# The destinations' rows of two message stages in a PSUM bank, and one bank for the transposes: a graph network kernel on one Trainium2 core

## The reference, cut to what matters

```python
# second layer (stage "msg1"): 16 features by 8 edge attributes
x_j = node_features[col]
m = jnp.einsum('ei,ej,ijh->eh', x_j, edge_attr_e3nn, W_msg_tp) * norm_msg_tp
m = jax.nn.silu(m)
m = m @ W_msg_lin * norm_lin
agg = jax.ops.segment_sum(m, row, num_segments=n_nodes)
...
# fourth layer (stage "msg3"): 16 attributes by 16 features
edge_mats = (edge_features @ kernel + bias).reshape(-1, d, d)
neighbors = node_features[pair_indices[:, 1]]
transformed = jnp.einsum('eij,ej->ei', edge_mats, neighbors)
aggregated = jax.ops.segment_sum(transformed, pair_indices[:, 0], num_segments=node_features.shape[0])
```

## Time and profile before

| | |
|---|---|
| median of three runs | 25,102.21 us (25,093.5 to 25,139.49) |
| the profiled execution's own time | 25,105.15 us |
| its span from first to last instruction | 25,103.4 us |
| granted TensorE clock over the span | 0.723 of 2.4 GHz |
| PE / PEld / DVE busy | 15,996.3 / 11,741.1 / 16,286.5 us |
| ACT / POOL busy | 3,853.7 / 18,136.2 us |
| stage msg1 | 9,523 to 12,890 us, 125 turns |
| stage msg3 | 20,834 to 24,655 us, 125 turns |

### The profile page before, as it was taken

The page is one execution under the profiler, slowest core; times in us unless marked ns, Lnnn a source line. Parts: engine busy times, 40 slices in busy tenths (PEclk is TensorE's granted clock), DMA queues, the critical chain, the costliest instruction groups (busy, mean ns, idle before and its releaser), DMA issues. The chain is left out here.

```text
span 25103.4 us, 351859 instructions
## 1 busy us (share of the span) xinstructions
PE 15996.3 (64%) x99053; PEld 11741.1 (47%) x99056; DVE 16286.5 (65%) x41450; ACT 3853.7 (15%) x8407; POOL 18136.2 (72%) x17443
## 2 busy tenths in 40 slices
PE   4211110266666647888853888888888838999993
PEld 3211110155555535666633454455545516777772
DVE  7679976177777726777761666666666645666664
ACT  0000000122222211111100111111111101222220
POOL 5777777677777737777753777777777767888884
PEclk7555555555555557888875889888888867888886
DMA  3211111011111101111120111111111120101012
GB/s 103 82 35 43 44 37 30 14 31 31 31 31 31 31 10 25 25 25 25 25 79 7 20 19 20 19 19 20 20 19 19 20 72 24 26 25 26 25 26 74
DMA packets 1007292, 810.94 MB, mean 32 GB/s; under 512 B 579829, under 2 KB 897503, under 8 KB 1003105
## 3 DMA queue, kind: packets, MB, share of 16 engines
q0 software_dynamic: 557728, 189.18, 6.0%
q1 hardware_dynamic: 348648, 290.30, 4.3%
q10 hardware_dynamic: 100800, 330.28, 3.4%
HBM read 414.80 MB, written 393.60 MB: 32 GB/s over the span
## 5 line engine op out<-in xcount | busy, mean ns | idle before, releaser
L1513 POOL DMA_INDIRECT msgs<-msg_msg,msg_pos x4875 | 5730.9, 1176 | 1550.8 <-issue 1485.0
L1748 POOL DMA_INDIRECT sheaf_got<-table,sheaf_idx x3125 | 3180.1, 1018 | 952.8 <-issue 952.8
L977 POOL DMA_INDIRECT gat_got<-table,gat_idx x3125 | 2963.5, 948 | 953.9 <-issue 952.1
L1410 PE MATMUL msg_dps<-msg_dhotq,msg_dleft 128*128 x16500 | 3517.4, 377 | 0.0
L1410 PE MATMUL sheaf_dps<-sheaf_dhotq,sheaf_dleft 128*128 x18000 | 3341.7, 343 | 0.9 <-DVE sheaf_dhotq L1393 0.9
L988 POOL DMA_INDIRECT ring<-table,src_all x2325 | 2217.2, 954 | 733.2 <-issue 707.9
L1410 PEld LDWEIGHTS msg_dps<-msg_dhotq,msg_dleft 128*128 x16500 | 1840.1, 116 | 1397.5 <-issue 650.2
L1319 PE MATMUL place_look_ps<-place_nexts,place_hot_at 98*128 98x128 f32 x5000 | 1624.0, 465 | 1330.4 <-DVE place_same L1224 929.5
L1410 PEld LDWEIGHTS sheaf_dps<-sheaf_dhotq,sheaf_dleft 128*128 x18000 | 1820.5, 102 | 1310.0 <-issue 260.0
L1622 ACT COPY msg_flip<-msg_fps 128x384 f32<-128x384 f32 (+1 forms) x3000 | 1357.7, 493 | 5281.3 <-PE msg_fps L1580 5272.3
L1756 POOL DMA_INDIRECT msgs<-sheaf_msg,sheaf_pos x1625 | 1787.9, 1100 | 519.7 <-issue 519.7
(11 more groups left out here) (463 smaller groups left out, 29550.8 us busy)
## 6 DMA issues: line engine op xcount, KB each, us to landing
msg_ex<-ex SPq DMA_DIRECT2D x250, 400.0 KB
gat_sums<-gat_acc ACTq DMA_DIRECT2D x125, 675.0 KB
msgs<-msg_msg,msg_pos POOLq DMA_INDIRECT x4875
tail_m<-msgs SPq DMA_DIRECT2D x75, 800.0 KB
src_sums<-tail_acc ACTq DMA_DIRECT2D x75, 800.0 KB
gat_sums<-gat_acc ACTq DMA_DIRECT2D x125, 425.0 KB
ring<-table,src_all POOLq DMA_INDIRECT x3125
ex<-zeros ACTq DMA_DIRECT2D x25, 2000.0 KB
```

The source lines that it names most:

```text
L977: pool.indirect_dma_start(got[b][:, j, :], None, table, bass.IndirectOffsetOnAxis(idx[b][:, j:j + 1], 0)).then_inc(gathered[b], 16)
L1410: last = pe.matmul(self.acc[:, n, 0:self.BQ], left, hot_q, start=False, stop=False, skip_group_check=True)
L1513: pool.indirect_dma_start(msgs, bass.IndirectOffsetOnAxis(pos[b][:, j:j + 1], 0), msg[b][:, j, :], None).then_inc(scattered[b], 16)
L1748: pool.indirect_dma_start(got[b][:, j, :], None, table3, bass.IndirectOffsetOnAxis(idx[b][:, j:j + 1], 0)).then_inc(gathered[b], 16)
```

## The change

The destinations' rows go to PSUM. One bank, `own_ps`, takes the place of the two SBUF buffers `own`; the last column is copied to an SBUF tile `carry`, from which the next turn's scans start. The 16 bias columns of msg3 stay in SBUF (`bias`), with a copy of their own. The bank comes from the transposes, which now have one, and so every batch of transposes waits until ACT has copied the one before. PE's order is written anew: the batches of the next group are laced with parts of the message products of this one, and the direct products stand behind the first batch of a turn and behind groups 2, 4 and 6.

```diff
-                own = [sb(f"{name}_own{b}", [P, CW, fills], F32, ctx) for b in range(2)]
+                carry = sb(f"{name}_carry", [P, fills], F32, ctx)
+                bias = [sb(f"{name}_bias{b}", [P, CW, fills - D], F32, ctx) for b in range(2)] if fills > D else None
...
-                flip_ps = [ctx.enter_context(nc.psum_tensor(f"{name}_fps{r}", [P, 512], F32)) for r in range(2)]
+                flip_ps = ctx.enter_context(nc.psum_tensor(f"{name}_fps", [P, 512], F32))
+                own_ps = ctx.enter_context(nc.psum_tensor(f"{name}_ops", [P, 512], F32))
+                own = own_ps[:, 0:CW * D].rearrange("p (t f) -> p t f", f=D)
...
                     def spread_own(i, b, turn, first):
...
+                        if not (first and b == 0):
+                            dve.wait_ge(outered, 2 * i)
+                            dve.wait_ge(carried, (2 if bias else 1) * i)
                         for f in range(fills):
-                            last = dve.tensor_tensor_scan(own[b][:, :, f], kp, ex[b][:, :, f], own[1 - b][:, CW - 1, f:f + 1],
-                                                          ALU.mult, ALU.add)
+                            to = own[:, :, f] if f < D else bias[b][:, :, f - D]
+                            last = dve.tensor_tensor_scan(to, kp, ex[b][:, :, f], carry[:, f:f + 1], ALU.mult, ALU.add)
                         last.then_inc(spread_, 1)
                         dve.wait_ge(spread_, i + 1)
+                        dve.tensor_copy(carry[:, 0:D], own[:, CW - 1, :]).then_inc(carried, 1)
+                        if bias:
+                            dve.tensor_copy(carry[:, D:fills], bias[b][:, CW - 1, :]).then_inc(carried, 1)
...
-                        mine = own[b][:, lo:hi, 0:D]
+                        mine = own[:, lo:hi, :]
...
+                    def turn_group(i, g, n, first):
+                        u = g * lots + n
+                        if not (first and u < 1):
+                            pe.wait_ge(copied, i * U + u)
+                        for k, t in enumerate(groups[g]):
+                            last = pe.transpose(flip_ps[:, k * P:(k + 1) * P],
+                                                outer[g // 4][:, t - parts[g // 4][0], n * P:(n + 1) * P], ident[:, :])
+                        last.then_inc(turned, 1)
...
                     def body(i, r, first):
                         pe.wait_ge(outered, 2 * i + 1)
-                        turn_group(i, 0, first)
+                        turn_group(i, 0, 0, first)
+                        direct(i, r, 0)
+                        for n in range(1, lots):
+                            turn_group(i, 0, n, first)
                         for g, ts in enumerate(groups):
-                            h, q = g // 4, g % 2
+                            pe.wait_ge(copied, i * U + (g + 1) * lots)
                             if g + 1 == 4:
                                 pe.wait_ge(outered, 2 * i + 2)
...
+                            for n in range(lots):
+                                if g + 1 < G:
+                                    turn_group(i, g + 1, n, first)
+                                multiply(i, g, first, len(ts) * n // lots, len(ts) * (n + 1) // lots)
+                                if g and n == lots - 1:
+                                    direct(i, r, g)
...
-                                act.copy(flip[q][n][:, 0:len(ts) * P], flip_ps[u % 2][:, 0:len(ts) * P]
+                                act.copy(flip[q][n][:, 0:len(ts) * P], flip_ps[:, 0:len(ts) * P]
```

More of the change, by code:

```diff
@@ L1477, in messages @@
                                                     for n in ("att_in", "ex_in", "pos_in", "scattered"))
-                spread_, outered, turned, copied, multiplied, done, asked, said, admitted, let_in, first_got, steps, start_steps = (
+                spread_, outered, turned, copied, multiplied, done, asked, said, admitted, let_in, first_got, steps, start_steps, carried = (
                     sem(f"{name}_{n}") for n in
                     ("spread", "outered", "turned", "copied", "multiplied", "done", "asked", "said", "admitted", "let_in",
-                     "first_got", "steps", "start_steps"))
+                     "first_got", "steps", "start_steps", "carried"))
                 block = ctx.enter_context(nc.Block())
@@ L1522, in _ @@
                     dve.wait_ge(first_got, 16)
-                    start.link(dve.tensor_copy(own[1][:, CW - 1, :], first_row[:, 0:fills]))
+                    start.link(dve.tensor_copy(carry[:, :], first_row[:, 0:fills]))
                     sums.vector_start(dve)
@@ L1534, in post @@
                                msg_ps[h][:, 0:(hi - lo) * D].rearrange("p (t f) -> p t f", f=D), work[h],
-                               own[b][:, lo:hi, :], asked, said).then_inc(done, 1)
+                               bias[b][:, lo:hi, :] if bias else None, asked, said).then_inc(done, 1)
                         dve.wait_ge(done, 2 * i + h + 1)
@@ L1573, in _ @@
                 def _(pe):
-                    def turn_group(i, g, first):
-                        for n in range(lots):
-                            u = g * lots + n
-                            if not (first and u < 2):
-                                pe.wait_ge(copied, i * U + u - 1)
-                            for k, t in enumerate(groups[g]):
-                                last = pe.transpose(flip_ps[u % 2][:, k * P:(k + 1) * P],
-                                                    outer[g // 4][:, t - parts[g // 4][0], n * P:(n + 1) * P], ident[:, :])
-                            last.then_inc(turned, 1)
+                    def turn_group(i, g, n, first):
[6 more added lines that the diff above has]
+                        last.then_inc(turned, 1)
@@ new lines, in multiply @@
+                    def multiply(i, g, first, lo, hi):
+                        h, q = g // 4, g % 2
+                        if g % 4 == 0 and lo == 0 and not first:
+                            pe.wait_ge(done, 2 * i - 1 + h)
+                        for k in range(lo, hi):
+                            c = groups[g][k] - parts[h][0]
+                            for n in range(lots):
+                                last = pe.matmul(msg_ps[h][:, c * D:(c + 1) * D], flip[q][n][:, k * P:(k + 1) * P],
+                                                 weights[n], start=(n == 0), stop=(n == lots - 1),
+                                                 skip_group_check=True)
+                        if hi == len(groups[g]):
+                            last.then_inc(multiplied, 1)
@@ L1584, in body, with direct @@
+                    def direct(i, r, g):
+                        if (not isinstance(i, int) or i > 1) and g % 2 == 0:
+                            sums.tensor(pe, i - 2, r, g // 2 * sums.cd // 4, (g // 2 + 1) * sums.cd // 4)
                     def body(i, r, first):
                         pe.wait_ge(outered, 2 * i + 1)
-                        turn_group(i, 0, first)
+                        turn_group(i, 0, 0, first)
+                        direct(i, r, 0)
+                        for n in range(1, lots):
+                            turn_group(i, 0, n, first)
@@ L1587, in body @@
                         for g, ts in enumerate(groups):
-                            h, q = g // 4, g % 2
+                            pe.wait_ge(copied, i * U + (g + 1) * lots)
                             if g + 1 == 4:
                                 pe.wait_ge(outered, 2 * i + 2)
-                            if g + 1 < G:
-                                turn_group(i, g + 1, first)
-                            pe.wait_ge(copied, i * U + (g + 1) * lots)
-                            if g % 4 == 0 and not first:
-                                pe.wait_ge(done, 2 * i - 1 + h)
@@ L1596, in body @@
-                            for k, t in enumerate(ts):
-                                c = t - parts[h][0]
-                                for n in range(lots):
-                                    last = pe.matmul(msg_ps[h][:, c * D:(c + 1) * D], flip[q][n][:, k * P:(k + 1) * P],
-                                                     weights[n], start=(n == 0), stop=(n == lots - 1),
-                                                     skip_group_check=True)
-                            last.then_inc(multiplied, 1)
@@ L1603, in body @@
-                            if not isinstance(i, int) or i > 1:
-                                if g % 2:
-                                    sums.tensor(pe, i - 2, r, g // 2 * sums.cd // 4, (g // 2 + 1) * sums.cd // 4)
+                            for n in range(lots):
+                                if g + 1 < G:
[3 more added lines that the diff above has]
+                                    direct(i, r, g)
```

2 lines of the change are left out of this document (1 added, 1 removed).

## The result

The changed kernel takes 26,137.68 us (median of three runs, 26,131.35 to 26,165.75) against 25,102.21: the ratio is 1.0411, with a 95% interval of 1.0388 to 1.0435. It is slower, as forecast, by 1,035 us where 1,400 were forecast. The profiled execution took 26,137.68 us over a span of 26,136.0, at a mean granted clock of 0.700 (0.723 before).

A forecast was written before the change was run, and what follows sets the result against it. POOL, never waiting, was taken to bound both stages, with DVE close behind in msg1 and PE in msg3. 25,105 + 260 (msg1) + 1,150 (msg3) = 26,515, said as 26,500 us; range 26,000 to 27,000, chance 0.55.

The forecast's parts named there:

- both of its mechanisms: msg1: a further column before the exponential DVE awaits, +260 us; msg3: one-bank gaps and low clock on PE, +1,150 us.
- Scatters near 1.0 us and POOL idle for `done`: Sign for both stages: POOL's mean scatter drops to near 1.0 us and POOL, which never waited before, waits.
- PE has only 0.2 us a turn to give in msg3: msg3: PE waits for DVE only 0.2 us a turn, so a free POOL could gain 25 us in all.
- DVE's copies and scans: DVE: one small copy a turn in msg1, two in msg3, 0.2 us each; PSUM scans and reads cost nothing.
- The further column: msg1, PE: 1.99 us of direct products before group 1's transposes, on DVE's path; the wait grows by 2.3 us.
- the lower of the two cases worked out: msg1: DVE's wait grows by 2.3 us, or by 4.2 if the added column of direct products runs at the low clock.
- DVE's own round: msg1: DVE's turn if left alone, 26.5 us, of which 6.25 wait for the exponential of half 1.
- msg3's gaps: msg3, PE: with one bank, waits between transpose batches total 3.1 us a turn in place of 0.5.
- msg3's clock: msg3, PE: stretches without direct products and columns behind them run at the low clock, 10.5 us a turn; was 3.7.
- The clock does not care about gaps: Rival 1, chance 0.28: gaps of 0.4 us leave the clock alone; msg3's turn 33.0 us, time 25,665 us.
- The clock stays up: Rival 2, chance 0.09 with rival 3: respread direct products remove the low clock; msg3's turn 29.3 us, time 24,905 us.
- the third rival: All of POOL's gain comes through, 3 and 5 us a turn, about -1,000 us: 24,100; chance 0.09 with rival 2.

## Why the prediction was right

Its direction and both of its mechanisms held; the sizes were too large by 360 us of 1,400.

- *POOL.* Scatters near 1.0 us and POOL idle for `done`: both seen. That this gain comes to nothing, since the engines behind are no quicker, held: the one-bank kernel with SBUF rows shows it (46 us at most). That PE has only 0.2 us a turn to give in msg3, read from the earlier trace rows, was a step that failed: the run with fewer scatters shows 1.4 us. A busy engine is not a bound if a low clock is what keeps it busy. The Trainium skill (SBUF — State Buffer, "Who interferes with whom") says that a DVE instruction with two SBUF inputs contends with a GpSimd instruction that reads SBUF. The trace agrees: with one input of the outer products in PSUM the long scatters of msg3 are gone (none above 1.35 us, 4.4 before).
- *DVE's copies and scans.* The copy takes 0.17 us, 0.2 assumed. A scan of msg3 into PSUM takes 260 ns and one into SBUF 253; the outer products keep their time. That is 0.1 us a turn, where nothing was assumed.
- *msg1.* DVE's waits were to go from 6.25 to near 8.5 us a turn and went to 8.2. The turn is 28.3 to 28.5 us where 29.0 was forecast, and the term is +154 in place of +260. The further column ran at the high clock, the lower of the two cases worked out. The prediction took DVE's own round as 26.5 us and gave all of the loss to the order of PE's work. Reckoned in the same way, with POOL out of the way, the round is 26.3, the order adds 1.8 us (2.3 forecast), and the bank 0.2, which the prediction had left out. The moved column shows the place: 140 of the 154 us come back. But the two-bank kernel with all scatters divides the loss into 79 for the order and 118 for the bank, less 43; the part that the bank plays in msg1 was not foreseen, and its size is open.
- *msg3's gaps.* 3.1 us a turn were forecast, and about 2.5 are lost (37.8 less 26.2 and the clock's 9.1). The count of batches was right and so was the distance of 1.1 to 1.2 us. It is smaller since, at the low clock, PE's own work fills the time of the copy: between 22033.58 and 22039.47 no row waits.
- *msg3's clock* was the step mis-sized most. 0.76 is 48% of 37.8 us at the low level and costs 9.1 us a turn; 10.5 were taken. The turns differ (38.6 us at 0.73 up to 22026.29, 33.9 at 0.85 behind it), so these are means of 118 turns of the trace. The stretches before the three places of direct products lose 3.0, 0.7 and 0.9 us to the low clock (2.6, 1.0 and 1.0 forecast). The column behind group 2 takes 3.81 us (3.87 forecast), the one behind group 4 3.03, since the clock is up there in part of the turns, and the pair 5.70, 1.7 us above the high clock's 3.98, where 2.4 was taken. So the clock falls where the prediction put it, and the second column and the pair were priced too high, by 0.9 and 0.7 us. Turn 37.8 for 39.8, term +869 for +1,150. The range given for the clock, 0.70 to 0.75, missed its 0.76 by little (0.75 over the whole stage).
- *The rivals.* "The clock does not care about gaps" fell: same order, two banks, 0.89, or 0.94 with POOL out of the way. "The clock stays up" fell too, with msg3 at 0.76, but its reason held: the columns spread anew do raise the clock (0.94 for 0.91), only the bank takes more than that. The whole of POOL's gain was 1,000 us in the third rival; with another order of PE's work the time did fall by 772 us (25,102 to 24,330). That rival was excluded for this change, not for the idea: PE's 26.2 us of plain work bound msg3 at 3,317 us, not at POOL's 24.8 x 125 = 3,100.
- The Trainium skill (TensorE: Matmul & The Clock Gate, "A second HAM failure mode: psum-queue depth-cycling") says that small idle steps between groups of matmuls let the clock swing. The traces agree as far as they go: in the same order the clock is 0.89 (0.94 with fewer scatters) with one such step a turn, and 0.76 with six or seven. But with the direct products in pairs as many steps left it at 0.95, and it fell at one place of the turn alone.

The sum of the misses: 106 us in msg1, 281 in msg3, less 12 us outside the two stages and 15 by which the forecast was rounded, is 360.

## What to carry to other kernels

Before a bank, a buffer or a port is given to the engine that never waits, count what the engine right behind it has to give: here POOL's turn in msg3 fell by 4.9 us (20 x 0.243), and PE had 1.4. Leave out some of the bound engine's work to measure that, since an engine at a low clock can look busier than it must be. A bank taken from PE's transposes opened gaps of some 0.3 us here that cost 2.5 us a turn by themselves, while the low clock cost 9.1, 5.4 more than before; read the granted clock by stretches, and put independent wide matmuls, cut into pieces as long as the gap, into each of them. If the order is right, the same trade that lost 4% wins 3%.

## What the runs showed of the hardware

- Transposes and narrow message products, with 1.2 us of gaps in 4.6 us, were followed by a stretch of 6.6 us at 1.2 GHz. With a piece of wide bf16 products at every second or third place (0.66 us each), the mean granted clock was 1.00 over 3,000 us.
- The same pieces two at a time, with gaps of some 0.2 to 0.7 us, had a clock of 0.95: it fell in 103 of 121 turns, each time at or near the end of the turn's first stretch, 3.5 us without wide products and with 0.9 us of waits in it. Shorter gaps with wide products in between did not bring it down.
- After a standstill of some 5 us in msg1 PE restarted at 0.50 and kept it for 4 us or more; how long differed between four kernels with the same order (8.12 to 8.69 us from the restart to DVE's request), and their msg1 with it (27.7 to 28.7 us a turn).
- Scans that write PSUM took 260 ns for 25 elements, those that write SBUF 253. DVE's operands in PSUM free POOL's scatters: over 3,000 us of msg3 these take 0.987 us in place of 1.232, in otherwise like kernels.
